# Value products of eight heads into both halves of one PSUM bank, with twelve probability slots and one transposed output buffer

## The chip, the cores and the metric

The kernel runs on one core of a Trainium2 chip. A core has five engines that each work through their own list of instructions in order: TensorE (PE, matmuls and transposes), VectorE (DVE), ScalarE (ACT), GpSimd (POOL) and SyncE (SP, which here only issues DMAs). They meet through semaphores. Matmul results land in PSUM, eight banks of 128 partitions x 512 float32; everything else is in the on-chip buffer. The metric is the time of one launch on the device in microseconds (us), lower is better.

## The reference

One post-norm decoder layer, 16 sequences of 256 tokens, width 256, 16 heads of 16:

```python
x = layernorm(x + self_attention(x))             # q, k RMS-normalised, rotary, causal softmax
x = layernorm(x + cross_attention(x, ctx))       # causal softmax, key mask
x = layernorm(x + ffn(x))                        # RMS norm, light (128) and heavy (1024) hidden units, gelu
# attention, per head:
attn = softmax(where(causal, -inf, q @ k.T * scale))
out  = attn @ v
```

The router of the feed-forward part selects 256 of 256 tokens, so every token goes through both paths, and the kernel computes them as nine chunks of 128 hidden units.

## The kernel before

All 16 sequences are run as a software pipeline, unrolled, one step per sequence. In step i the self-attention (called 1) of sequence s = i, the cross-attention (called 2) of c = i-1, the tail of the cross-attention of f = i-2 and the feed-forward of l = i-3 are in flight together. PE's list of a step has four phases of 16 heads each, and `phase` (line 590) places other work before head h of a phase ("position h"):

- **S1** and **S2**: `scores(1, s, h)` and `scores(2, c, h)`, scores with queries on the partitions, from which DVE takes the row maxima (L869).
- **T1** and **T2**: `scores_t(1, s, h)` and `scores_t(2, c, h)`, the transposed scores less the maxima. Each head fills a bank of a ring of three. ACT takes the exponential (L728) into `pr`, POOL zeroes the masked triangle there (L1176), and PE multiplies the result by the values.

The product is `values(a, b, gr)` (line 508): four heads at a time, each on its own strip of 32 columns of the array, so that the four output strips fill the 128 partitions of `bank3`. It uses columns 0 to 255 of the bank, first the upper keys (256 columns), then the lower keys (128 columns), and a float32 matmul shows as two records in the trace, so that a group of four heads is 16 records. ACT copies a finished group into `oT` (`copy_group`, 256 columns wide), and the next group waits for that copy. Then `out_tokens` transposes `oT` back, DVE divides by the softmax sums (`normalise_heads`, L906 and L909, into `on`), `out_dims` transposes `on` (L367), ACT copies it into `onT`, and `out_proj` applies the output weights. From there DVE adds the residual (L918), takes statistics (L925 to L931), POOL takes the root (L1166), DVE writes the normalised `x` (L946).

Positions of this kernel: the groups 0, 1 and 2 stand at positions 7, 11 and 15 of T1 and T2; group 3 of the self-attention stands at position 2 of T2, behind `k2` (position 1); group 3 of the cross-attention at position 3 of the next S1, behind `transpose_x1` (position 1) and ahead of `q2` (position 4). `out_tokens` follows at position 4 (self) and 5 (cross), `out_dims` at 8 and 10, `out_proj` at 10 and 12. `pr` has eight slots; ACT's exponential of head h waits until the group that read the slot last is done. ACT's list holds, among the exponentials of T1, a copy of `xnh` after head 13 (L674), and among those of T2 the copy of `nat2k` before head 3, of `onT` before head 9, and the squares of the next q and k (L815) before heads 5 and 10. DVE splits q and k of the cross-attention into three bfloat16 parts (L853, L856, L858, tiles `rest` and `nat2`): k just ahead of `normalise_heads(1)`, q ahead of head 5 of the maxima in S1, with `normalise_heads(2)` ahead of head 7. POOL takes the root for `x1` between the masks of heads 12 and 13 of T2.

Of the kernel before, what the change touches and what calls it, by code (L numbers as in the profile page):

```python
# [56 lines left out]
NG = H // HG  # L57
FCH = 9
# [5 lines left out]
def build(nc, io):  # L64
# [4 lines left out]
    with ctx:  # L69
# [51 lines left out]
        pr = sb("pr", [P, 2 * HG, 3 * P])  # L121
        oT = [None] + [sb(f"oT{a}", [P, NG, T]) for a in (1, 2)]
# [89 lines left out]
        def iterations(step):  # L212
            for i in range(-2, B + 4):
# [3 lines left out]
                 if 0 <= turn[2] < B]  # L217
        RING = (0, 1, 2)
# [121 lines left out]
        def _(pe):  # L340
# [89 lines left out]
            def hidden(b, j):  # L430
# [9 lines left out]
                elif j == 1:  # L440
                    if live(b + 1):
                        pe.wait_ge(s_oT[2], NG * (b + 2))
# [41 lines left out]
            def transpose_max(a, b):  # L484
# [3 lines left out]
                else:  # L488
                    if live(b - 3):
                        pe.wait_ge(s_g, FCH * (b - 3) + LIGHT)  # L490
                    if live(b - 2):
                        pe.wait_ge(s_oT[2], NG * (b - 1))
                    wait(pe, s_oT[1], NG * b)
# [14 lines left out]
            def values(a, b, gr):  # L508

                pe.wait_ge(s_prob[a], H * b + HG * (gr + 1))  # L510
                if gr == 0:
# [3 lines left out]
                    elif live(b + 1):  # L515
                        pe.wait_ge(s_oT[1], NG * (b + 2))
# [5 lines left out]
                for key in range(2):  # L522
                    for j in range(HG):
                        h = HG * gr + j
                        out = bank[OT_BANK][VW * j:VW * (j + 1), :]
                        if key == 0:
                            mm(out[:, 0:T], v[:, 0, h, :], pr[:, h % (2 * HG), 0:T], True, False, True)
                        else:
                            last = mm(out[:, P:T], v[:, 1, h, :], pr[:, h % (2 * HG), T:3 * P], False, True, True)
                last.then_inc(s_pv[a], 1)  # L530

            def out_tokens(a, b):

                pe.wait_ge(s_oT[a], NG * (b + 1))
                for t in range(TT):
# [26 lines left out]
                    for gr in range(NG):  # L562
                        last = nc.tensor.transpose(bank[TOK_BANK[a][t]][:, gr * P:(gr + 1) * P],
                                                   oT[a][:, gr, t * P:(t + 1) * P], idf[:, :])
# [33 lines left out]
            def step(i):  # L598
# [9 lines left out]
                if live(f):  # L608
                    add(OUT2_AT[0], values, 2, f, NG - 1)
# [37 lines left out]
                if live(s):  # L647
                    add(K2_AT, k2, s)
                    add(OUT1_AT[0], values, 1, s, NG - 1)
# [11 lines left out]
                if live(c):  # L661
                    for gr in range(NG - 1):
                        add(HG * gr + VALUES_AFTER, values, 2, c, gr)
# [8 lines left out]
        def _(act):  # L672
# [3 lines left out]
            def copy_v(a, b):  # L676
                act.wait_ge(s_v[a], b + 1)

                wait(act, s_pv[a], NG * (b - 1) if a == 1 else NG * b)
# [12 lines left out]
            def copy_group(a, b, gr):  # L692
                act.wait_ge(s_pv[a], NG * b + gr + 1)

                wait(act, s_ott[a], TT * b)
                copy(oT[a][:, gr, :], bank[OT_BANK][:, 0:T]).then_inc(s_oT[a], 1)
# [19 lines left out]
            def exponential(a, b, h):  # L716
                act.wait_ge(s_st[a], H * b + h + 1)

                if h >= 2 * HG:
                    act.wait_ge(s_pv[a], NG * b + h // HG - 1)  # L720
                elif a == 1:
                    wait(act, s_pv[2], NG * (b - 1) - 2 + h // HG + 1)
                    wait(act, s_pv[1], NG * b)
                elif live(b + 1):
                    act.wait_ge(s_pv[1], NG * (b + 1) + 3 + h // HG)
                else:
                    act.wait_ge(s_pv[2], NG * (b - 1) + 3 + h // HG)
                nc.scalar.activation(pr[:, h % (2 * HG), :], ring_bank("T", a, b, h)[:, 0:3 * P], ACT.Exp, scale=HD ** -0.5)\  # L728
# [24 lines left out]
            def step(i):  # L753
                s, c, f, l = i, i - 1, i - 2, i - 3

                if live(f):
# [555 lines left out]
```

## Time and profile before

| | |
|---|---|
| median of 3 runs | 1029.55 us (1028.53 to 1033.22) |
| profiled execution | 1031.08 us, of which the span of the profile is 1029.3 us |
| PE busy | 921.1 us, 89% |
| DVE busy | 734.1 us, 71% |
| ACT busy | 490.1 us, 48% |
| POOL busy | 466.4 us, 45% |

The span is what the profile covers from its first to its last instruction. Busy is the union of an engine's instructions. The ends of matmuls are modelled, and they overlap in the pipeline of the array; how long a stretch of matmuls holds the engine is read from the start of its first matmul to the start of the matmul behind it. A name like `L342` is the line of a helper through which nearly all matmuls go, so matmuls are told apart by their tiles: `pr,va1a`, `pr,va1b` (self) and `pr,va` (cross) are the value products, `ctxT,wk` is `k2`, `x1T,wq` is `q2`, `idf,x` is `transpose_x1`, `idf,oT` is `out_tokens`, `idf,on` is `out_dims`, `wo,onT` is `out_proj`, `stk1q,stk1k` and `stk2q,stk2k` are `scores_t`, `stk1k,stk1q` and `stk2k,stk2q` with `cmaskb,idb` are `scores`.

### The profile page before, as it was taken

How to read it: one execution, taken by the hardware profiler on the slowest of the kernel's cores; microseconds unless marked ns; L12 is line 12 of the kernel's file. 1: busy time of each engine (PE TensorE's matmuls, PEld its weight loads, DVE VectorE, ACT ScalarE, POOL GpSimd, SP SyncE). 2: the span in 40 equal slices, each digit the busy share in tenths (PEclk: the TensorE clock that was granted, in tenths of full speed). 3: DMA queues.
4: the chain of work that ended last, by engine and by line, in shares of the span. 5: the costliest groups of instructions: out<-in, count | busy, mean ns of one | idle time of the engine just before them, and what ended most of it. 6: DMA issues, size and time to landing. Idle time of an engine off the chain costs nothing.

```text
span 1029.3 us, 21587 instructions
## 1 busy us (share of the span) xinstructions
PE 921.1 (89%) x7776; PEld 711.1 (69%) x7776; DVE 734.1 (71%) x1843; ACT 490.1 (48%) x1047; POOL 466.4 (45%) x883
## 2 busy tenths in 40 slices
PE   2565898899999999999999999999999999998886
PEld 2333565587877778786878777787868786766675
DVE  8645858687787877777878878777777788563612
ACT  1131161645555564636465555546374655445343
POOL 2150454545546363546455564635464554233221
PEclk9666799999999999999999999999999999999989
DMA  3629356554729183554546280937556462804000
GB/s 104 82 70 148 63 63 79 79 74 70 97 48 106 39 107 61 81 87 64 84 75 93 52 116 24 110 57 89 79 64 95 62 85 47 111 13 64 21 1 21
DMA packets 79643, 74.22 MB, mean 72 GB/s; under 512 B 8592, under 2 KB 78896, under 8 KB 79536
## 3 DMA queue, kind: packets, MB, share of 16 engines
q1 hardware_dynamic: 75872, 68.90, 46.6%
q10 hardware_dynamic: 3664, 3.94, 1.7%
q8 instruction: 62, 1.02, 0.5%
q14 instruction: 45, 0.37, 0.2%
HBM read 17.49 MB, written 4.20 MB: 21 GB/s over the span
## 4 chain that ended last, share of the span: by engine, by line
PE 61%; DVE 17%; issue 9%; POOL 4%; ACT 3%; DMA 3%; ACTq 1%; SPq 0%; POOLq 0%; DVEq 0%
PE bank L342 56%; PE bank L367 4%; DVE mx L869 3%; POOL pr L1176 3%; DMA y<-in_b 2%; ACT pr L728 2%; DVE x L946 1%; DVE rest L853 1%; DVE y L918 1%; DVE st L925 1%; DVE ss L971 1%; DVE nat2q L858 1%; DVE on L909 1%; DVE rden L906 1%; ACT sq L815 1%
## 5 line engine op out<-in xcount | busy, mean ns | idle before, releaser
L728 ACT ACTIVATE pr<-bank 128x384 f32<-128x384 f32 x512 | 242.5, 499 | 205.5 <-PE bank L342 205.2
L869 DVE TENSOR_REDUCE mx<-bank 128x3 f32<-128x384 f32 x512 | 268.6, 552 | 92.8 <-PE bank L342 89.2
L1176 POOL TENSOR_SCALAR_AFFINE_SELECT pr<-pr 128x256 f32<-128x256 f32 x512 | 225.3, 448 | 214.6 <-ACT pr L728 210.8
L342 PE MATMUL bank<-w,g 128*128 128x256 f32 x576 | 170.8, 389 | 1.1 <-ACT g L740 1.1
L342 PE MATMUL bank<-cmaskb,idb 128*128 128x256 bf16 x512 | 145.7, 285 | 28.5 <-DMA stk1k<-nat1k 14.6
L740 ACT ACTIVATE g<-bank,b 128x256 f32<-128x256 f32 x144 | 68.3, 475 | 112.3 <-PE bank L342 111.8
L1200 POOL TENSOR_TENSOR xTlow<-xT,xThigh 128x512 fp32r<-128x512 f32 x16 | 21.2, 1327 | 174.7 <-ACT xThigh L674 174.7
L342 PEld LDWEIGHTS bank<-w,g 128*128 128x128 f32 x576 | 89.6, 190 | 5.2 <-ACT g L740 1.5
L342 PE MATMUL bank<-stk1k,stk1q 97*128 97x128 bf16 (+1 forms) x512 | 88.6, 259 | 0.0
L342 PEld LDWEIGHTS bank<-cmaskb,idb 128*128 128x128 bf16 x512 | 50.4, 98 | 52.6 <-DVE mx L869 22.2
L342 PE MATMUL bank<-stk1q,stk1k 100*128 100x256 bf16 (+1 forms) x512 | 79.9, 254 | 4.5 <-DMA stk1q<-mT 3.1
L342 PE MATMUL bank<-stk2k,stk2q 97*128 97x128 bf16 (+1 forms) x512 | 82.3, 246 | 0.0
L342 PE MATMUL bank<-stk2q,stk2k 100*128 100x256 bf16 (+1 forms) x512 | 74.8, 251 | 1.9 <-ACT pr L728 0.9
L246 POOL TENSOR_TENSOR qc<-qn,ropeC 128x256 f32<-128x256 f32 x60 | 49.9, 831 | 50.0 <-DVE qn L998 32.6
L342 PE MATMUL bank<-xnh,w1h 128*128 128x256 f32 x288 | 69.1, 321 | 2.3 <-DVE y L918 2.1
L342 PEld LDWEIGHTS bank<-stk1q,stk1k 100*128 100x128 bf16 x512 | 42.3, 100 | 38.3 <-ACT pr L728 8.6
L342 PE MATMUL bank<-wo,onT 128*128 128x256 f32 x256 | 63.3, 391 | 2.5 <-ACT onT L674 2.5
L342 PEld LDWEIGHTS bank<-stk2k,stk2q 97*128 97x128 bf16 x512 | 50.5, 99 | 20.8
L1166 POOL TENSOR_TENSOR rstd<-ve,minus_half 128x2 f32<-128x2 f32 x48 | 33.4, 695 | 63.1 <-DVE ve L931 63.1
L342 PE MATMUL bank<-pr,va 128*32 128x256 f32 (+1 forms) x1024 | 56.7, 340 | 5.5 <-POOL pr L1176 5.3
L342 PEld LDWEIGHTS bank<-stk1k,stk1q 97*128 97x128 bf16 x512 | 53.5, 104 | 9.9 <-issue 0.3
L674 ACT ACTIVATE oT<-bank 128x256 f32<-128x256 f32 x128 | 49.9, 390 | 20.4 <-PE bank L342 14.6
(143 smaller groups left out, 1792.1 us busy)
## 6 DMA issues: line engine op xcount, KB each, us to landing
stk1q<-nat1q SPq DMA_DIRECT2D x96, 128.0 KB, 4.7
stk1k<-nat1k SPq DMA_DIRECT2D x96, 128.0 KB, 6.7
stk2k<-nat2k SPq DMA_DIRECT2D x96, 128.0 KB, 4.6
stk2q<-nat2q SPq DMA_DIRECT2D x96, 128.0 KB, 6.1
xT<-in_xT SPq DMA_DIRECT2D x16, 256.0 KB, 2.8
x<-in_x SPq DMA_DIRECT2D x16, 256.0 KB, 6.8
ctxT<-in_ctxT SPq DMA_DIRECT2D x16, 256.0 KB, 3.0
out_x<-x SPq DMA_DIRECT2D x16, 256.0 KB, 6.5
```

The lines of the kernel that those rows point to most:

```text
L246: ops.tensor_tensor(qc[:, t, s * D:(s + 1) * D].rearrange("p (h d) -> p h d", d=HD), qn[:, t, s * D:(s + 1) * D].rearrange("p (h d) -> p h ...
L342: return nc.tensor.matmul(out, lhsT, rhs, start=start, stop=stop, skip_group_check=check)
L367: last = nc.tensor.transpose(bank[k][:, c * T + t * P:c * T + (t + 1) * P], src[:, t, c * P:(c + 1) * P], idf[:, :])
L674: return nc.scalar.activation(out, in_, ACT.Copy)
L728: nc.scalar.activation(pr[:, h % (2 * HG), :], ring_bank("T", a, b, h)[:, 0:3 * P], ACT.Exp, scale=HD ** -0.5)\
L740: nc.scalar.activation(g[:, j, :], bank[HIDDEN_BANK[j % 2]][:, 0:T], ACT.Gelu, bias=b1[:, j:j + 1])\
L815: nc.scalar.activation(sq[:, t, :], bank[QK1_BANK[t]][:, :], ACT.Square).then_inc(s_sq, 1)
L853: V.tensor_tensor(rest[:, :], bank[SPLIT_BANK[a][s]][:, :], n[:, 0, :], ALU.subtract)\
L869: V.tensor_reduce(mx3[:, h, :], scored[:, 0:3 * P].rearrange("p (k t) -> p k t", k=3), AX.X, ALU.max, negate=True).then_inc(s_mx[a], 1)
L1166: G.tensor_tensor(out, base, minus_half[:, 0:w], ALU.pow)\
L1176: G.affine_select(out=slot, in_=slot, compare_op=ALU.is_ge, fill=0.0, base=0, pattern=[[0, 2], [1, P]], channel_multiplier=-1).then_inc(s_ ...
L1200: G.tensor_tensor(xTp[1][:, :, :], xT[:, :, :], xTp[0][:, :, :].bitcast(f32), ALU.subtract)\
```

## The change

`values` now takes eight heads ("a part"): two groups of four, the second into columns 256 to 511 of the same bank, with one wait ahead of both and one semaphore step behind both. `copy_part` copies a part in one instruction of 512 columns. Part 0 stands at position 11 of T1 and T2, part 1 where group 3 stood. `pr` has twelve slots that are handed out round robin over all T phases, and `oT` is one buffer for both attentions. ACT copies part 0 ahead of head 14 of T1 and of head 13 of T2, and part 1 where it copied group 3. No matmul is added or left out.

```diff
+GH = 2
+SLOTS = 12
-        pr = sb("pr", [P, 2 * HG, 3 * P])
-        oT = [None] + [sb(f"oT{a}", [P, NG, T]) for a in (1, 2)]
+        pr = sb("pr", [P, SLOTS, 3 * P])
+        oT = sb("oT", [P, NG, T])
+        turns_t = [turn[1:] for turn in turns if turn[0] == "T"]
+        def slot(a, b, h):
+            return pr[:, (H * turns_t.index((a, b)) + h) % SLOTS, :]
+        def wait_slot(eng, a, b, h):
+            tile = H * turns_t.index((a, b)) + h - SLOTS
+            if tile >= 0:
+                a0, b0 = turns_t[tile // H]
+                eng.wait_ge(s_pv[a0], GH * b0 + tile % H // (H // GH) + 1)
...
-            def values(a, b, gr):
-                pe.wait_ge(s_prob[a], H * b + HG * (gr + 1))
-                if gr == 0:
+            def values(a, b, part):
+                pe.wait_ge(s_prob[a], H * b + H // GH * (part + 1))
+                if part == 0:
...
-                    pe.wait_ge(s_oT[a], NG * b + gr)
+                    pe.wait_ge(s_oT[a], GH * b + part)
...
+                for gr in range(NG // GH):
+                    for key in range(2):
+                        for j in range(HG):
+                            h = H // GH * part + HG * gr + j
+                            out = bank[OT_BANK][VW * j:VW * (j + 1), gr * T:(gr + 1) * T]
...
-                    add(OUT2_AT[0], values, 2, f, NG - 1)
+                    add(OUT2_AT[0], values, 2, f, 1)
...
-                    for gr in range(NG - 1):
-                        add(HG * gr + VALUES_AFTER, values, 1, s, gr)
+                    add(VALUES_AFTER[0], values, 1, s, 0)
...
+            def copy_part(a, b, part):
+                act.wait_ge(s_pv[a], GH * b + part + 1)
+                if a == 1:
+                    wait(act, s_ott[2], TT * (b - 1))
+                    wait(act, s_ott[1], TT * b)
+                else:
+                    wait(act, s_ott[2], TT * b)
+                    wait(act, s_ott[1], TT * (b + 2) if live(b + 1) else TT * B)
+                groups = slice(part * (NG // GH), (part + 1) * (NG // GH))
+                copy(oT[:, groups, :], bank[OT_BANK][:, :].rearrange("p (g t) -> p g t", g=NG // GH)).then_inc(s_oT[a], 1)
...
-                        if h % HG == 0 and h >= 2 * HG:
-                            copy_group(1, s, h // HG - 2)
+                        if h == COPY_HALF_AT[0]:
+                            copy_part(1, s, 0)
...
-VALUES_AFTER = 7
+VALUES_AFTER, COPY_HALF_AT = (11, 11), (14, 13)
```

The change moves PE's instructions in three kinds of place. The first is S1, on PE, between the transposes of `x1` and `q2` (tiles `x1T`, `wq2`). Before:

```order
L342 MATMUL bank3<-pr,va2 32x256 [waits outT_copied2,probs_ready2]
L342 MATMUL bank3<-pr,va2 32x256 x3
L342 MATMUL bank3<-pr,va2 32x128 x4
L342 MATMUL bank0<-cmaskb,idb 128x2x128 [waits max_ready1]
L342 MATMUL bank0<-stk1k,stk1q 128x128
L342 MATMUL bank0<-stk1k,stk1q 128x256
L342 MATMUL bank6<-x1T,wq2 128x256 [waits x1T_copied]
L342 MATMUL bank6<-x1T,wq2 128x256 x3
```

The same place on PE now, with part 1 of the cross-attention:

```order
L356 MATMUL bank3<-pr,va2 32x256 [waits outT_copied2,probs_ready2]
L356 MATMUL bank3<-pr,va2 32x256 x3
L356 MATMUL bank3<-pr,va2 32x128 x4
L356 MATMUL bank3<-pr,va2 32x256 x4
L356 MATMUL bank3<-pr,va2 32x128 x4
L356 MATMUL bank0<-cmaskb,idb 128x2x128 [waits max_ready1]
L356 MATMUL bank0<-stk1k,stk1q 128x128
L356 MATMUL bank0<-stk1k,stk1q 128x256
L356 MATMUL bank6<-x1T,wq2 128x256 [waits x1T_copied]
L356 MATMUL bank6<-x1T,wq2 128x256 x3
```

Eight more value matmuls, of heads 8 to 11, stand ahead of `q2`.

The second place is the end of T1 on PE, from head 14 to `k2` (tiles `ctxT`, `wk2`). Before:

```order
L342 MATMUL bank0<-stk1q,stk1k 128x256 [waits exp_ready1]
L342 MATMUL bank0<-stk1q,stk1k 128x128
L342 MATMUL bank3<-pr,va1b 32x256 [waits outT_copied1,probs_ready1]
L342 MATMUL bank3<-pr,va1b 32x256 x3
L342 MATMUL bank3<-pr,va1b 32x128 x4
L342 MATMUL bank1<-stk1q,stk1k 128x256 [waits exp_ready1]
L342 MATMUL bank1<-stk1q,stk1k 128x128
L342 MATMUL bank2<-stk2q,stk2k 128x256 [waits exp_ready1,max_loaded2]
L342 MATMUL bank2<-stk2q,stk2k 128x128
L342 MATMUL bank5<-ctxT,wk2 128x256 [waits dve_rest1,ctxT_loaded]
```

The same place on PE now:

```order
L356 MATMUL bank0<-stk1q,stk1k 128x256 [waits exp_ready1]
L356 MATMUL bank0<-stk1q,stk1k 128x128
L356 MATMUL bank1<-stk1q,stk1k 128x256 [waits exp_ready1]
L356 MATMUL bank1<-stk1q,stk1k 128x128
L356 MATMUL bank2<-stk2q,stk2k 128x256 [waits exp_ready1,max_loaded2]
L356 MATMUL bank2<-stk2q,stk2k 128x128
L356 MATMUL bank5<-ctxT,wk2 128x256 [waits dve_rest1,ctxT_loaded]
```

Group 2 is gone from between heads 14 and 15; its heads are now in part 1, behind `k2`.

The third place is T2 on PE, from head 6 to `out_dims` (tiles `idf`, `on1`). Before:

```order
L342 MATMUL bank2<-stk2q,stk2k 128x256 [waits exp_ready2]
L342 MATMUL bank2<-stk2q,stk2k 128x128
L342 MATMUL bank3<-pr,va2 32x256 [waits outT_copied1,va_ready2,probs_ready2]
L342 MATMUL bank3<-pr,va2 32x256 x3
L342 MATMUL bank3<-pr,va2 32x128 x4
L342 MATMUL bank0<-stk2q,stk2k 128x256 [waits exp_ready2]
L342 MATMUL bank0<-stk2q,stk2k 128x128
L367 MATMUL bank5<-idf,on1 128x128 [waits dve_rest2,on_ready1]
```

The same place on PE now:

```order
L356 MATMUL bank2<-stk2q,stk2k 128x256 [waits exp_ready2]
L356 MATMUL bank2<-stk2q,stk2k 128x128
L356 MATMUL bank0<-stk2q,stk2k 128x256 [waits exp_ready2]
L356 MATMUL bank0<-stk2q,stk2k 128x128
L381 MATMUL bank5<-idf,on1 128x128 [waits dve_rest2,on_ready1]
```

Group 0 is gone from ahead of `out_dims`; its heads are in part 0, at position 11, behind `out_proj`.

## Rows read from the trace of the kernel before

**Rows 1.** The page: the span.

```profile
span 1029.3 us, 21587 instructions
```

**Rows 2.** Windows: stretch, its length, busy us and counts by engine, PE clock, DMA.

```profile
489.24:498.66 9.42, 8.82 (x82) 7.48 (x82) 8.53 (x20) 4.90 (x9) 7.86 (x14) 1.00 0.80 117
498.66:518.70 20.04, 20.04 (x153) 17.08 (x154) 15.03 (x37) 6.91 (x13) 5.85 (x8) 1.00 0.45 80
```

**Rows 3.** Waits of PE in one step, 489 to 545.4: us, times, longest.

```profile
PE bank L367 <- DVE on L909: 0.6, 1, 0.6
PE bank L367 <- DVE x L946: 0.4, 1, 0.4
```

**Rows 4.** The chain that ended last, from 480 to 560: start, us, what.

```profile
482.92 0.60 ACT sq L815
...
489.24 0.66 PE bank L367 x4
489.90 3.74 PE bank L342 x36
...
494.14 0.69 DVE rest L853
...
498.66 0.66 PE bank L367 x4
```

**Rows 5.** Timeline of PE around one group of four heads.

```profile
466.03 0.33 PE L342 MATMUL bank<-stk1q,stk1k 100*128 100x256 bf16 x2
466.29 0.86 PE L342 MATMUL bank<-pr,va1b 128*32 128x256 f32 x16
466.53 0.62 PE L342 MATMUL bank<-pr,va1b 128*32 128x256 f32 x12
467.08 0.34 PE L342 MATMUL bank<-stk1q,stk1k 100*128 100x256 bf16 x2
467.25 0.65 PE L342 MATMUL bank<-w,g 128*128 128x256 f32 x2
```

**Rows 6.** Timeline from head 11 of T1 to head 2 of T2.

```profile
470.10 0.34 PE L342 MATMUL bank<-stk1q,stk1k 100*128 100x256 bf16 x2
471.87 0.63 ACT L674 ACTIVATE xnh<-bank 128x512 fp32r<-128x512 f32 x1
472.35 0.92 ACT L728 ACTIVATE pr<-bank 128x384 f32<-128x384 f32 x2
472.95 0.79 POOL L1176 TENSOR_SCALAR_AFFINE_SELECT pr<-pr 128x256 f32<-128x256 f32 x2 [0.47 <-ACT pr L728]
474.67 0.86 PE L342 MATMUL bank<-pr,va1b 128*32 128x256 f32 x16
475.46 0.34 PE L342 MATMUL bank<-stk2q,stk2k 100*128 100x256 bf16 x2
```

**Rows 7.** Timeline of T2, and of S1 from group 3 to `q2`.

```profile
475.83 0.49 ACT L728 ACTIVATE pr<-bank 128x384 f32<-128x384 f32 x1 [0.57 <-PE bank L342]
476.22 0.59 ACT L674 ACTIVATE nat2k<-bank 128x512 bf16<-128x512 f32 x1
480.03 0.66 PE L367 MATMUL bank<-idf,on 128*128 128x128 f32 x4
487.13 0.69 POOL L1166 TENSOR_TENSOR rstd<-ve,minus_half 128x2 f32<-128x2 f32 x1
488.35 0.84 DVE L946 TENSOR_SCALAR x<-y,mv,rstd 128x256 f32<-128x256 f32 x2
490.38 0.86 PE L342 MATMUL bank<-pr,va 128*32 128x256 f32 x16
491.46 1.89 PE L342 MATMUL bank<-x1T,wq 128*128 128x256 f32 x8
```

**Rows 8.** Groups of ACT's instructions: busy us, mean ns, idle before.

```profile
L674 ACT ACTIVATE oT<-bank 128x256 f32<-128x256 f32 x128 | 49.9, 390 | 20.4 <-PE bank L342 14.6 <-issue 5.7
L674 ACT ACTIVATE onT<-bank 128x512 f32<-128x512 f32 x32 | 18.9, 592 | 7.3 <-PE bank L367 7.3
```

More of the change, by code:

```diff
@@ L441, in hidden @@
                     if live(b + 1):
-                        pe.wait_ge(s_oT[2], NG * (b + 2))
+                        pe.wait_ge(s_oT[2], GH * (b + 2))
                     else:
@@ L491, in transpose_max @@
                     if live(b - 2):
-                        pe.wait_ge(s_oT[2], NG * (b - 1))
-                    wait(pe, s_oT[1], NG * b)
+                        pe.wait_ge(s_oT[2], GH * (b - 1))
+                    wait(pe, s_oT[1], GH * b)
                 for t in range(TT):
@@ L515, in values @@
                     elif live(b + 1):
-                        pe.wait_ge(s_oT[1], NG * (b + 2))
+                        pe.wait_ge(s_oT[1], GH * (b + 2))
                     elif live(b - 2):
@@ L519, in values @@
                 else:
-                    pe.wait_ge(s_oT[a], NG * b + gr)
+                    pe.wait_ge(s_oT[a], GH * b + part)
                 v = values_of(a, b)
[L522 to L529, printed above, removed]
+                for gr in range(NG // GH):
[3 more added lines that the diff above has]
+                            out = bank[OT_BANK][VW * j:VW * (j + 1), gr * T:(gr + 1) * T]
+                            if key == 0:
+                                mm(out, v[:, 0, h, :], slot(a, b, h)[:, 0:T], True, False, True)
+                            else:
+                                last = mm(out[:, P:T], v[:, 1, h, :], slot(a, b, h)[:, T:3 * P], False, True, True)
                 last.then_inc(s_pv[a], 1)
             def out_tokens(a, b):
-                pe.wait_ge(s_oT[a], NG * (b + 1))
+                pe.wait_ge(s_oT[a], GH * (b + 1))
                 for t in range(TT):
@@ L648, in step @@
                     add(K2_AT, k2, s)
-                    add(OUT1_AT[0], values, 1, s, NG - 1)
+                    add(OUT1_AT[0], values, 1, s, 1)
                 if live(i + 2):
@@ L661, in step @@
                 if live(c):
-                    for gr in range(NG - 1):
-                        add(HG * gr + VALUES_AFTER, values, 2, c, gr)
+                    add(VALUES_AFTER[1], values, 2, c, 0)
                 phase((lambda h: scores_t(2, c, h)) if live(c) else None, others)
@@ L677, in copy_v @@
                 act.wait_ge(s_v[a], b + 1)
-                wait(act, s_pv[a], NG * (b - 1) if a == 1 else NG * b)
+                wait(act, s_pv[a], GH * (b - 1) if a == 1 else GH * b)
                 copy(values_of(a, b)[:, :, :, 0:HD], bank[V_BANK[a]][:, :].rearrange("p (t h d) -> p t h d", t=TT, h=H))\
@@ L690, in copy_out @@
                 copy_dims(onT[a], DIM_BANK[a]).then_inc(s_onT[a], 1)
[L692 to L696, printed above, removed]
+            def copy_part(a, b, part):
[3 more added lines that the diff above has]
+                    wait(act, s_ott[1], TT * b)
+                else:
+                    wait(act, s_ott[2], TT * b)
+                    wait(act, s_ott[1], TT * (b + 2) if live(b + 1) else TT * B)
+                groups = slice(part * (NG // GH), (part + 1) * (NG // GH))
+                copy(oT[:, groups, :], bank[OT_BANK][:, :].rearrange("p (g t) -> p g t", g=NG // GH)).then_inc(s_oT[a], 1)
             def copy_x1(b):
@@ L717, in exponential @@
                 act.wait_ge(s_st[a], H * b + h + 1)
[L719 to L728, printed above, removed]
+                wait_slot(act, a, b, h)
+                nc.scalar.activation(slot(a, b, h), ring_bank("T", a, b, h)[:, 0:3 * P], ACT.Exp, scale=HD ** -0.5)\
                     .then_inc(s_exp[a], 1)
@@ L754, in step @@
                 s, c, f, l = i, i - 1, i - 2, i - 3
-                if live(f):
-                    copy_group(2, f, NG - 2)
                 if live(c):
@@ L760, in step @@
                 if live(f):
-                    copy_group(2, f, NG - 1)
+                    copy_part(2, f, 1)
                 if live(c):
@@ L796, in step @@
                         if h == COPY1_AT[2]:
-                            copy_group(1, s, NG - 1)
+                            copy_part(1, s, 1)
                         if h == COPY1_AT[3]:
@@ L803, in step @@
                     if live(c):
-                        if h % HG == 0 and h >= 2 * HG:
-                            copy_group(2, c, h // HG - 2)
+                        if h == COPY_HALF_AT[1]:
+                            copy_part(2, c, 0)
                         exponential(2, c, h)
```

8 lines of the change are left out of this document (3 added, 5 removed).

## The prediction

> **What bounds the kernel now.** I read the chain of waits first. In the steady part it alternates between PE and short passages through the other engines [rows 4]. The windows then show how unevenly PE is loaded: from `out_dims` of the cross-attention in S1 to the start of T1 it is busy for 20.04 of 20.04 us, while from `transpose_x1` (489.24) to that `out_dims` (498.66) it is busy for 8.82 of 9.42 us [rows 2]. The list of waits names where it stands still: once per step for `on` (0.6 us) and once for `x` (0.4 us) [rows 3]. So the step consists of stretches that PE sets, and of stretches that a chain through ACT, DVE and POOL sets, in which PE has as much work as the chain lasts and no more. The change moves PE work between these stretches. What it is worth has to be read stretch by stretch, and the reader is to look for which of them lose work and which gain it. The clock is at its upper level, 2.4 GHz (granted 1.00), in both stretches [rows 2].
>
> **What one merge is worth on PE.** A group of four heads starts 0.26 us after the score tile ahead of it (466.03 to 466.29), where such a tile otherwise holds PE for 0.17 (467.08 to 467.25), so entering costs 0.09. The next tile starts 0.79 after the group's first matmul [rows 5]. Inside, the first pass over 256 columns takes 0.24 (466.29 to 466.53). I take 0.22 for the second and half of that for each of the two passes over 128 columns: 0.24 + 0.22 + 0.11 + 0.11 = 0.68, and the remaining 0.11 are the exit. Four heads more, put behind without entry and exit, need 2 x 0.22 + 2 x 0.11 = 0.65. A part therefore holds PE for 0.79 + 0.65 = 1.44 us behind its entry, or 1.53 with it; two groups take 2 x 0.88 = 1.76. A merge gives 0.23 us, and there are 4 per step and 64 in all. Bounds: below, that the second four heads take a full 0.88; above, 0.65. I take 0.65, since all its passes stand in the group already.
>
> The Trainium skill (TensorEngine Tiling (Array Packing), Key Properties) says that changing the tiling mode drains the array. The gaps of 0.09 and 0.11 at a group's edges agree with that [rows 5]. By that rule alone half of the mode changes would go, and the kernel would get faster; this is the first rival below.
>
> **X1 to `out_dims` in S1: one group becomes one part.** The chain runs from `transpose_x1` over PE's list (36 records of L342, among them group 3 at 490.38 and `q2` at 491.46) to the split of q on DVE at 494.14 and over `normalise_heads` to `out_dims` at 498.66 [rows 4, 7]. PE takes its list in order: everything in part 1 stands ahead of `q2`. Behind `q2`, ACT's `nat2q`, DVE's split, two maxima, two reciprocals and two multiplications follow as a chain, and `out_dims` waits for its end (0.6 us [rows 3]), as it did. So `q2` moves back by 0.65 us, and `out_dims` with it: the wait for `on` stays, since its two sides move together. Behind it comes the stretch in which PE is full [rows 2]; nothing there takes the delay back. Cost: +0.65 per step. ACT's copy of the part (0.59 instead of 0.39 by [rows 8]) lies beside `q2` (1.89 us [rows 7]) and costs nothing.
>
> **T1 and the head of T2: two merges and group 2 moved, gain about zero.** PE reaches head 11 of T1 at 470.10 behind two groups [rows 6]; behind one part it does so 0.23 earlier, 469.87. Then comes `transpose_xn`, and heads 12 to 15 without the group that filled PE between 14 and 15. These tiles go through a ring of three banks, so PE is now tied to ACT. An exponential starts 0.37 behind its tile (475.46 to 475.83 [rows 6, 7]), ends 0.49 later, and ACT starts one about every 0.37 to 0.39 when it is full (475.83 to 476.22). Counting on from 469.87: exponential 11 at 470.25, 12 at 470.88 (its tile stands behind a tile of 0.17 and `transpose_xn`, four transposes that I put at 0.45 after the 0.66 of such four with their modelled end [rows 4]), 13 at 471.25, `xnh` at 471.62, the copy of part 0 at 472.10 (a 512-wide copy holds ACT for 0.48, 471.87 to 472.35 [rows 6]), exponentials 14 and 15 at 472.58 and 472.95. The mask of 15 ended 0.47 behind its exponential (472.35 + 0.92 = 473.27 against 472.95 + 0.79 = 473.74 [rows 6]); now it ends at about 473.95. PE's last tile of T1 waits for exponential 12, the first of T2 for 13, until 471.80; `k2`, as long as `q2` without its modelled end, holds it for about 1.8, to 473.75, and part 1 can start at 474.0. Group 3 stood at 474.67 [rows 6]. The part ends 1.44 later, and head 2 of T2 starts at 475.45 to 475.48 where it started at 475.46 [rows 6]. The merges (0.46) and the earlier start are used up by waits of PE for the ring (about 0.6). Bounds from both sides: PE without any such wait would be there 0.46 earlier; with the mask of head 15 late by one more mask it would be there 0.4 later. I take 0.
>
> **T2 to `out_dims`: group 0 goes, nothing is gained.** Head 2 of T2 at 475.46 releases exponential 2, that is followed in ACT's list by `nat2k` at 476.22, and this by the split of k on DVE, then `normalise_heads`, and `out_dims` starts at 480.03 [rows 6, 7]: 4.57 us of chain. PE reached `out_dims` just then because group 0 (0.88) filled the time. Without it PE stands there for about 0.9 us. The transposes of `oT` at position 4 now wait for a copy of 0.59 behind `nat2k`, 0.08 more than PE has time for; the chain over DVE covers that, and I take 0.02.
>
> **T2 to X1: 0.** From `out_dims`, `qk1` for the next sequence but one goes to the squares on ACT at 482.92, and from there over DVE (the sums, the residual, statistics, Newton steps) to `x` at 488.35 and the transposes at 489.24 [rows 4, 7]. PE had groups 1 and 2 in that time (1.76) and waited 0.4; it has part 0 (1.53), waits about 0.6, and the chain is as long. One step of it moves: head 12 comes 0.65 later behind the larger part, ACT has no copy between exponentials 11 and 12 any more (0.26), and POOL's root, behind the mask of head 12, would end at about 488.2 instead of 487.82 [rows 7]. DVE is ready for `x` at 488.35. That cover is 0.1 us thick; if it is gone each step pays up to 0.3.
>
> **Sum.** 0.65 + 0 + 0.02 + 0 = 0.67 us per step. Steps 2 to 16 have the S1 stretch, 15 times: 10.0 us. At both ends of the program the phases stand alone; a part more on the last chain costs 0.65, a copy less ahead of the loads of the feed-forward weights gives about that back. I take 0.4 together. The profiled execution was 1031.08 us for a span of 1029.3 [rows 1], so the changed one would be 1041.5. That execution lies 1.5 above the median of the three runs; against the median the forecast is 1040.0.
>
> **Rivals.**
> First, the merges show in full: PE is the busiest engine and 64 x 0.23 = 14.7 us go, 1014.8 us. For it speaks that PE is full over 20 us of each step; against it, that no group stands in those 20 us, and that every group that goes stands ahead of a chain that PE waits for anyway. Chance 0.07.
> Second, the ends of T1 and T2 give back what S1 pays: if the chain at the end of T1 is looser than I counted, so that PE is 0.46 ahead at head 2 of T2, that goes through the chain behind it whole. Then 0.67 - 0.46 = 0.2 per step, or 3 us; with a shortened split of q (it runs beside POOL's rotation and is stretched by it) also nothing. 1027 to 1034, centre 1031. Chance 0.12.
> Third, one more wait takes hold: POOL's root for `x1` comes late by the full 0.3, and the mask of head 15 by 0.4, so that `x` and part 1 move. It decides as soon as exponential 12 of T2 starts later than about 486.7. Then 1.3 to 1.4 per step, 1051. Chance 0.09.
> Within my own case lies that the merge gives nothing inside the array: 0.88 instead of 0.65 in S1, 1043.5.
>
> **Chances and range.** My case has 0.72, its own range 1036 to 1045. The range that is to hold the time 8 times in 10 is 1033 to 1047: it takes in a small part of the second and of the third rival. A measurement of this kernel tells from no change what is more than about 0.5%, 5.1 us, so 1024.4 to 1034.7 is the same. Slower by more: 0.72 + 0.09 = 0.81, less a little for the low end of my case, 0.80. Same: 0.13. Faster: 0.07.
>
> **What would show it.** In the changed profile: from `transpose_x1` to `out_dims` 10.07 instead of 9.42 us; a step of 57.1 instead of 56.4 us; a part with 1.44 us from its first matmul to the next tile; PE's wait for `on` at two places per step, the new one in T2 near 0.9; its wait for `x` near 0.6 instead of 0.4 or a like time for exponential 13 just ahead; new waits for `pr` of ACT at the end of T1, 0.4 to 0.6 in sum; PE busy for less and ACT for about 64 x 0.19 = 12 us less, without a gain. I am wrong if the stretch from the first tile of T1 to head 2 of T2 is shorter than now by more than 0.2 us, if PE waits less for `on` in S1 than now, or if a stretch in which it is full gets shorter.

## The result and the profile after

The changed kernel takes 1053.26 us (median of 3 runs, 1052.33 to 1053.41) against 1029.55 us before (1028.53 to 1033.22). The ratio is 1.0219, with a 95% interval of 1.0179 to 1.0259. It is slower, as forecast, but by 23.7 us and not by 10.4, and outside the range. Whether it is slower by 2% or more the interval leaves open. Both profiled executions, 1053.26 and 1031.08 us, differ by 22.2 us, and so do their spans; the working below goes by these.

The page's span, which answers to [rows 1]:

```profile
span 1051.5 us, 21397 instructions
```

A steady step, from the transposes of `x1` to the next, takes 57.62 us instead of 56.41. The windows of the changed kernel cut one such step at `transpose_x1`, `out_dims` in S1, the first tile of T1, `k2`, head 2 of T2, `out_dims` in T2 and the next `transpose_x1`. The columns are those of [rows 2], and the first two lines answer to them:

```profile
496.80:507.06 10.26, 9.47 (x97) 7.92 (x97) 8.93 (x20) 5.09 (x9) 8.70 (x16) 1.00 0.96 122
507.06:527.09 20.03, 20.03 (x152) 17.08 (x153) 15.02 (x37) 6.93 (x13) 5.16 (x7) 1.00 0.37 72
527.09:537.21 10.12, 9.44 (x89) 6.64 (x88) 8.43 (x22) 6.92 (x15) 6.72 (x15) 1.00 0.02 4
537.21:540.69 3.48, 3.48 (x44) 2.48 (x42) 2.42 (x7) 2.32 (x6) 1.75 (x5) 1.00 0.66 121
540.69:545.26 4.57, 3.83 (x30) 2.73 (x26) 3.04 (x8) 3.34 (x8) 2.42 (x4) 1.00 1.15 124
545.26:554.42 9.16, 8.72 (x81) 6.70 (x82) 6.57 (x22) 5.75 (x14) 4.50 (x11) 1.00 0.61 66
```

The same cuts of the kernel before, behind those of [rows 2]:

```profile
518.70:529.05 10.35, 10.23 (x105) 6.97 (x104) 8.60 (x23) 7.72 (x18) 7.11 (x15) 1.00 0.02 4
529.05:531.87 2.82, 2.82 (x29) 2.00 (x26) 2.33 (x7) 1.79 (x5) 1.31 (x4) 1.00 0.43 104
531.87:536.45 4.58, 4.35 (x46) 3.15 (x42) 3.04 (x8) 3.25 (x8) 2.80 (x6) 1.00 1.16 125
536.45:545.65 9.20, 8.80 (x83) 6.62 (x81) 6.83 (x22) 5.98 (x15) 4.71 (x12) 1.00 0.72 80
```

| stretch | forecast | measured |
|---|---|---|
| `transpose_x1` to `out_dims` in S1 | +0.65 | +0.84 |
| `out_dims` to T1 | 0 | -0.01 |
| T1 to `k2` | about -0.65 | -0.23 |
| `k2` to head 2 of T2 | about +0.65 | +0.66 |
| head 2 to `out_dims` in T2 | +0.02 | -0.01 |
| `out_dims` to the next `transpose_x1` | 0 | -0.04 |
| step | +0.67 | +1.21 |

Two terms are off: S1 by 0.2 us, and T1 by 0.4. The reader is to see in the third line that PE's busy time in T1 fell by 0.79 us while the stretch fell by 0.23: the rest became waiting. The waits of PE in that step (496.8 to 554.4), which answer to [rows 3], name it:

```profile
PE bank L381 <- DVE on L916: 1.3, 2, 0.8
PE bank L356 <- ACT pr L739: 0.8, 3, 0.3
PE bank L356 <- POOL pr L1183: 0.3, 1, 0.3
```

The chain of waits over S1, which answers to [rows 4], shows the first term as one number. PE's piece behind `transpose_x1` was 3.74 us with 36 records and is 4.39 with 52, that is 0.65 longer:

```profile
496.80 0.66 PE bank L381 x4
497.46 4.39 PE bank L356 x52
...
502.35 0.69 DVE rest L860
503.06 0.64 DVE nat2q L863
...
507.06 0.66 PE bank L381 x4
```

The wait for `on` now stands at two places, 0.79 us in S1 (ahead of 507.06) and 0.48 in T2 (ahead of 545.26), and the one for `x` is gone. The wait of 0.3 for POOL's mask is new in T1. The timeline of the changed kernel at the end of T1, which answers to [rows 5, 6]; its three masks are those of heads 5, 6 and 7, behind POOL's root:

```profile
531.14 0.69 POOL L1173 TENSOR_TENSOR rr<-ssm,minus_half 128x2 f32<-128x2 f32 x1
531.79 1.75 POOL L1183 TENSOR_SCALAR_AFFINE_SELECT pr<-pr 128x256 f32<-128x256 f32 x3
533.60 1.51 PE L356 MATMUL bank<-pr,va1a 128*32 128x256 f32 x32 [0.29 <-POOL pr L1183]
535.04 0.34 PE L356 MATMUL bank<-stk1q,stk1k 100*128 100x256 bf16 x2
536.58 0.34 PE L356 MATMUL bank<-stk1q,stk1k 100*128 100x256 bf16 x2 [0.25 <-ACT pr L739]
537.21 1.94 PE L356 MATMUL bank<-ctxT,wk 128*128 128x256 f32 x8
539.25 1.51 PE L356 MATMUL bank<-pr,va1a 128*32 128x256 f32 x32
540.69 0.34 PE L356 MATMUL bank<-stk2q,stk2k 100*128 100x256 bf16 x2
```

And the kernel before at that place, with groups 0 and 1 and the same three masks:

```profile
522.72 0.86 PE L342 MATMUL bank<-pr,va1a 128*32 128x256 f32 x16
522.75 0.70 POOL L1166 TENSOR_TENSOR rr<-ssm,minus_half 128x2 f32<-128x2 f32 x1
523.40 1.76 POOL L1176 TENSOR_SCALAR_AFFINE_SELECT pr<-pr 128x256 f32<-128x256 f32 x3
525.74 0.86 PE L342 MATMUL bank<-pr,va1a 128*32 128x256 f32 x16
```

A part holds PE for 1.44 us, as worked out (533.60 to 535.04). Part 0 has to wait for the mask of head 7, as group 1 had. Before, that mask ended at 525.16, which is 6.47 us behind the first tile of T1 (518.69), and group 1 began 0.58 later. In the changed kernel it ends at 533.54, 6.45 behind the first tile of T1 (527.09): it did not move. But with group 0 gone from ahead, PE is there 0.83 us earlier, counted in the same way (its wait left out). The cover is used up, and 0.29 are waited. Part 1 starts 0.25 us nearer to `out_dims` of S1 than group 3 did, where 0.67 was forecast.

### The profile page after: what moved, and what is told of

Read it like the earlier page. It is cut to its first block, busy times and chain, and to the rows that moved or that the text cites. A ratio compares the mean times of both kernels' runs of the same rounds, so it can differ in the third digit from the quotient of the medians.

```text
span 1051.5 us, 21397 instructions
## 1 busy us (share of the span) xinstructions
PE 927.4 (88%) x7776; PEld 718.8 (68%) x7776; DVE 735.1 (70%) x1843; ACT 485.4 (46%) x983; POOL 460.4 (44%) x883
## 4 chain that ended last, share of the span: by engine, by line
PE 50%; DVE 24%; issue 11%; POOL 5%; ACT 3%; DMA 2%; ACTq 1%; SPq 0%; POOLq 0%; DVEq 0%
PE bank L356 45%; DVE mx L876 5%; PE bank L381 5%; POOL pr L1183 3%; DVE x L953 2%; DVE rest L860 2%; DMA y<-in_b 2%; DVE on L916 1%; DVE rden L913 1%; DVE y L925 1%; DVE st L932 1%; ACT pr L739 1%; POOL rr L1173 1%; DVE nat2q L863 1%; DVE ss L978 1%
## 5 line engine op out<-in xcount | busy, mean ns | idle before, releaser
L739 ACT ACTIVATE pr<-bank 128x384 f32<-128x384 f32 x512 | 232.7, 501 | 224.4 <-PE bank L356 221.5
L1183 POOL TENSOR_SCALAR_AFFINE_SELECT pr<-pr 128x256 f32<-128x256 f32 x512 | 220.7, 446 | 234.2 <-ACT pr L739 232.7
L356 PE MATMUL bank<-wo,onT 128*128 128x256 f32 x256 | 66.6, 406 | 2.5 <-ACT onT L687 2.5
L260 POOL TENSOR_TENSOR qc<-qn,ropeC 128x256 f32<-128x256 f32 x60 | 46.5, 775 | 48.7 <-DVE qn L1005 30.9
L356 PEld LDWEIGHTS bank<-stk2q,stk2k 100*128 100x128 bf16 x512 | 38.1, 99 | 38.0 <-issue 19.1
L356 PE MATMUL bank<-xnl,w1h 128*128 128x256 f32 x288 | 57.9, 283 | 0.0
```

Source lines behind the costliest of these rows:

```text
L260: ops.tensor_tensor(qc[:, t, s * D:(s + 1) * D].rearrange("p (h d) -> p h d", d=HD), qn[:, t, s * D:(s + 1) * D].rearrange("p (h d) -> p h ...
L356: return nc.tensor.matmul(out, lhsT, rhs, start=start, stop=stop, skip_group_check=check)
L739: nc.scalar.activation(slot(a, b, h), ring_bank("T", a, b, h)[:, 0:3 * P], ACT.Exp, scale=HD ** -0.5)\
L1183: G.affine_select(out=diagonal, in_=diagonal, compare_op=ALU.is_ge, fill=0.0, base=0, pattern=[[0, 2], [1, P]], channel_multiplier=-1).the ...
```

## The experiments

Steps are from one `transpose_x1` to the next in the steady part. Times are medians with their range, ratios are to the kernel before.

**Slots and buffer without a merge.** The changed kernel with four groups:

```diff
-GH = 2
+GH = 4     # positions 7, 11, 15 and copies as before; 12 slots, one oT
```

> Twelve slots and the one transposed output buffer alone: the products stay in groups of four at positions 7, 11, 15 and behind, with copies of 256 columns. Theory 1 (the loss comes from where the eight-head parts stand in PE's list): time of before, 1029 to 1031 us, a step of 56.4 us. Rival (the shared buffer or the slots bring a wait of their own): 1040 to 1053 us, with new waits of ACT for the oT or pr tiles.

Measured: 1029.74 us (1027.6 to 1034.09), ratio 1.0004 (0.9988 to 1.002), step 56.41. Slots and buffer cost nothing that these runs can tell; the loss belongs to the parts.

**Parts in the self-attention alone.**

```diff
-GH = 2
+GH = (None, 2, 4)     # parts for the self-attention, groups for the other
```

> Parts of eight heads for the self-attention alone, the cross-attention in groups of four. Theory 1: only the end of T1 and the head of T2 change, where the changed kernel loses 0.40 us per step (wait for the mask of head 7, waits for the ring of three banks at heads 15 and 0), so 0.4 x 14 = 5.6, 1035 us, and a stretch from the transposes of x1 to out_dims in S1 of 9.42 as before. Rival (losses of the two attentions are one loss, for instance of the wide copies on ACT): about half of 23.7, 1041 us.

Measured: 1040.39 us (1035.73 to 1041.45), ratio 1.0093 (1.0063 to 1.0122); the profiled execution has 1035.73. The step is 56.83, +0.42, and S1 is 9.41, unchanged: step and stretch are as theory 1 has them, while the median lies 5 us above its 1035, at the 1041 of the rival. The execution of 1035.73 had a mean granted clock of 0.956, the three of 1040 to 1041 had 0.946 to 0.952, so the time as a whole can't decide between the two expectations, and the step does.

**Parts in the cross-attention alone.**

```diff
-GH = 2
+GH = (None, 4, 2)
```

> Parts of eight heads for the cross-attention alone. Theory 1: the stretch from the transposes of x1 to out_dims in S1 grows from 9.42 to 10.26 (0.65 for four heads more ahead of q2, 0.19 because DVE's split of q then meets POOL's rotation), T2 stays within 0.1, and the last two steps, which have no qk1 and v1 to fill PE, lose 1 to 2 us each: 0.8 x 13 + 4 = 14 to 18, 1043 to 1048 us. Rival (half of the total each): 1041 us.

Measured: 1049.22 us (1043.61 to 1049.98), ratio 1.0175 (1.0143 to 1.0208), step 57.24, +0.83, with 10.29 from `transpose_x1` to `out_dims`; the time is 1 us above the forecast 1043 to 1048. The two halves add up to 1.25 per step, the whole change has 1.21. So there are two separate costs: T1 with the head of T2, and S1.

**`q2` ahead of the part in S1.**

```diff
-X1T_AT, OUT2_AT, Q2_AT = 1, (3, 5, 10, 12), 4
+X1T_AT, OUT2_AT, Q2_AT = 1, (4, 5, 10, 12), 3
     # ACT copies nat2q ahead of the part
```

> The changed kernel with q2 at position 3 of S1 and part 1 behind it at position 4, and on ACT the first bfloat16 part of q copied ahead of the part's copy. Theory 1 (the split of q is a chain that starts at q2, and part 1 ahead of it delays it): the stretch to out_dims falls from 10.26 to about 9.5, where PE's own work fills it, the wait for on at that place goes from 0.8 to under 0.2, and the time falls by 0.7 x 15 = 10, to 1042 us. Rival (that stretch is long because PE has more work in it): no change, 1053 us, and the stretch stays at 10.2.

Measured: 1058.5 us (1053.87 to 1059.53), ratio 1.0269 (1.0239 to 1.0298), step 58.05: a miss, the wrong way. `q2` did start 1.35 us behind `transpose_x1` instead of 2.87, but DVE's list holds the split of q behind the maximum of head 4, whose score tile now stands behind the part. The split's first step came 5.95 us behind `transpose_x1`, where it was 5.55.

**The same with the split one maximum earlier, and the same two edits in the kernel before.**

```diff
-QN_AT, NORM2_AT, SPLITQ_AT, ... = (1, 2), 7, 5, ...
+QN_AT, NORM2_AT, SPLITQ_AT, ... = (1, 2), 7, 4, ...
```

> As the run before (q2 at position 3 of S1, part 1 at 4), and DVE's split of q one head earlier, ahead of the maximum of head 4, whose score tile stands behind part 1 in PE's list. Theory 1 (the delay of out_dims in S1 comes from everything that stands ahead of the split of q in the lists of PE and DVE): now neither the part nor a score tile behind it is ahead of the split; the stretch from the transposes of x1 to out_dims falls from 10.68 in the run before, and from 10.29 in the changed kernel, to 9.5 to 9.7, and the time to about 1053 - 0.7 x 13 = 1044 us. Rival (DVE and POOL set that stretch by their own work, not by order): it stays at 10.2 to 10.7 and the time at 1053 to 1058.

> The same three edits in the kernel before: q2 ahead of group 3 of the cross-attention, its first part copied ahead of the group, the split of q ahead of the maximum of head 4. Theory 1: the wait of 0.6 for on goes in each step, the stretch falls from 9.42 to 8.8 to 9.0, the step from 56.41 to 55.9, the time to 1022 to 1024 us. Rival (the split, meeting POOL's rotation earlier, is stretched by as much): 1028 to 1031 us.

Measured in the changed kernel: 1051.91 us (1046.27 to 1053.76), ratio 1.0216 (1.0186 to 1.0246), step 57.56, S1 10.25. In the kernel before: 1026.03 us (1022.97 to 1027.79), ratio 0.9958 (0.9939 to 0.9976), step 56.33, S1 9.40. PE's waits in one step, first of the changed kernel so edited, then of the kernel before so edited:

```profile
PE bank L356 <- ACT pr L739: 0.8, 3, 0.3
PE bank L381 <- DVE on L916: 0.5, 1, 0.5
PE bank L578 <- ACT oT L687: 0.3, 1, 0.3
PE bank L356 <- POOL pr L1183: 0.3, 1, 0.3
```

```profile
PE bank L367 <- DVE x L946: 0.4, 1, 0.4
PE bank L342 <- POOL pr L1176: 0.2, 1, 0.2
```

In both the wait for `on` in S1 is gone, and in both the stretch is as long as it was (10.25 against 10.26, 9.40 against 9.42). So S1 has a second bound that lies just under the first: PE's own list, with a wait for the copy of `x1T` ahead of the weights of the earlier `q2` (0.36), and in the changed kernel one for the copy of the part (0.34). The part lengthens both. The reordering did not give the expected time back in either kernel: the changed one keeps its stretch, as the rival of its expectation has it, and the other gets 0.08 us per step where 0.5 was expected. The kernel before with it is the fastest of all that ran.

**POOL's rotation cut to 2 of 16 heads, in both kernels.** Part of the computation is left out in both: the rotary products of 14 heads.

```diff
-    ops.tensor_tensor(qc[:, t, s * D:(s + 1) * D] ..., ropeC ... [P, H, HD], ALU.mult)
+    ops.tensor_tensor(qc[:, t, s * D:s * D + 2 * HD] ..., ropeC ... [P, 2, HD], ALU.mult)
     # and the other products and the sum likewise
```

> The changed kernel with POOL's rotation of the next q and k cut to 2 of 16 heads (the rest of qc, of the rotated halves and of qr is left out, in all but the first sequence). If DVE's split of q is stretched because POOL's rotation runs beside it, the cast of nat2q falls from 640 ns to 430 and the subtraction from 1100 to 690, and the stretch to out_dims from 10.29 to about 9.7, so a step of 57.0 instead of 57.6. Rival (the 0.2 beyond the four heads come from PE or ACT): both keep their length, and the stretch stays at 10.3.

> The kernel before with POOL's rotation cut to 2 of 16 heads (part of the computation is left out), as the baseline for the same cut in the changed kernel, where the step lost 0.31 us and the split of q fell from 1100 to 693 ns. Theory 1 (in the changed kernel the split of q runs beside the rotation in a stretch in which it did not before): here the second half of the split falls too, since it met the rotation before, by 0.4, but the cast of nat2q is at 0.43 already and stays; x to out_dims is 0.4 shorter at most, that is the changed kernel lost nothing in this stretch that the cut gives back to it alone except the 0.2 of the cast. Rival (the rotation costs both kernels alike): step lower by 0.3, the same as in the changed kernel, and the difference of the two steps stays at 1.2 us.

Measured, one execution each: in the changed kernel 1049.78 us, step 57.31 (-0.31), S1 9.94; in the kernel before 1032.36 us, step 56.72 (+0.31), S1 9.72. Less work on POOL makes the kernel before slower, which neither theory of the second run expected. The durations of DVE's two steps of the split say why. Each line gives minimum, median and maximum in ns; first the kernel before, whole and with the light rotation, then the changed kernel, whole and with it:

```profile
L856 DVE CAST nat2q<-rest x16: 427/428/651, 109.6 to 945.3; 128x512 bf16<-128x512 f32 x16
L858 DVE TENSOR_TENSOR nat2q<-rest,nat2q x16: 693/1101/1103, 110.3 to 945.8; 128x512 bf16<-128x512 f32 x16
```

```profile
L858 DVE CAST nat2q<-rest x16: 426/1147/1149, 107.2 to 946.1; 128x512 bf16<-128x512 f32 x16
L860 DVE TENSOR_TENSOR nat2q<-rest,nat2q x16: 691/693/694, 107.6 to 946.5; 128x512 bf16<-128x512 f32 x16
```

```profile
L863 DVE CAST nat2q<-rest x16: 426/640/658, 108.5 to 965.0; 128x512 bf16<-128x512 f32 x16
L865 DVE TENSOR_TENSOR nat2q<-rest,nat2q x16: 693/1100/1104, 109.2 to 965.5; 128x512 bf16<-128x512 f32 x16
```

```profile
L865 DVE CAST nat2q<-rest x16: 426/716/726, 106.3 to 960.2; 128x512 bf16<-128x512 f32 x16
L867 DVE TENSOR_TENSOR nat2q<-rest,nat2q x16: 691/693/693, 106.7 to 960.6; 128x512 bf16<-128x512 f32 x16
```

With the light rotation both subtractions fall to 693 ns, but the casts grow, since another instruction of POOL now stands beside them. In the kernel before the cast grows by 0.72 us and the subtraction falls by 0.41, which is the 0.31 that the step lost; in the changed kernel they are +0.08 and -0.41, and the step fell by 0.31. Now S1 can be worked out for both pairs. The cast differs by 640 - 428 = 0.21 us between the whole kernels, and 0.65 for the four heads ahead of `q2` plus 0.21 makes 0.86; measured 0.84. It differs by 716 - 1147 = -0.43 between the light ones: 0.65 - 0.43 = 0.22; measured 9.94 - 9.72 = 0.22. So the 0.65 of the prediction fits both pairs, and the term that was missing is the length of DVE's cast, which depends on what POOL runs beside it. The first expectation had the subtraction right and the cast wrong.

**Part 0 of T1 one head later.**

```diff
-VALUES_AFTER, COPY_HALF_AT = (11, 11), (14, 13)
-MAX2_AT, XNT_AT = 5, 12
+VALUES_AFTER, COPY_HALF_AT = (12, 11), (14, 13)
+MAX2_AT, XNT_AT = 5, 13
```

> The changed kernel with part 0 of the self-attention one head later, at position 12 of T1, and the transposes of xn at 13. Theory 1 (T1 loses 0.29 by the wait for the mask of head 7, and more by the ring at heads 15 and 0): the mask is done by then, the wait of 0.29 goes, part 1 starts 0.3 earlier, the step is 57.3, and the time 1053 - 0.3 x 13 = 1049 us. Rival (the end of T1 is set by ACT's exponentials alone): the wait goes but comes back in the ring waits, 1053 us.

Measured: 1048.86 us (1044.64 to 1050.6), ratio 1.0174 (1.0142 to 1.0206), step 57.28, -0.34; PE's wait for the mask is gone, as theory 1 has it.

**POOL's root out of the way of that mask.**

```diff
-RR2_AT, RSTD3_AT, RSTD1_AT = 5, 3, 13
+RR2_AT, RSTD3_AT, RSTD1_AT = 8, 3, 13
```

> The changed kernel with POOL's root for k of the cross-attention (RR2_AT) between the masks of heads 7 and 8 of T1 instead of 4 and 5, so that the mask of head 7 is not behind it. Theory 1 (the covers at the end of T1): part 0 of T1 loses its wait of 0.3 us for the mask of head 7, and with it the stretch from x to x loses 0.3: step 57.3 instead of 57.63, and steps 14 and 15, where the same kind of wait stands ahead of part 0, lose at most as much; time lower by 3.5 to 5, 1048.5 to 1050. Rival (PE is tied to the ring of three tiles in any case, so that the wait is only the first of several in a row): the wait for the mask goes and those for ACT's exponentials grow by the same 0.3; step 57.55 to 57.65, time within 1 us of the changed kernel.

Measured: 1050.49 us (1046.18 to 1053.69), ratio 1.0208 (1.0183 to 1.0234), step 57.29. The time as a whole moved by less than its own spread, and its median is 0.5 us above what theory 1 had; the step, which repeats to 0.04 in each trace, decides. PE's waits in it:

```profile
PE bank L381 <- DVE on L916: 1.3, 2, 0.8
PE bank L356 <- ACT pr L739: 0.8, 3, 0.3
```

The wait of 0.3 went and no other one grew, so it was on the path in full, and theory 1 holds for the step. Here the mask of head 7 ends 5.64 us behind the first tile of T1, not 6.47: the root was what had held it. About the same 0.33 to 0.34 comes back by moving the part behind the mask or the root behind the mask.

**One merge in T1 only.** The stretches in which the cross-attention's parts cost are left as before, and the one merge stands in T1, where PE was busy for 10.23 of 10.35 us:

```diff
+PARTS = (None, ((0, 4), (4, 12), (12, 16)), ((0, 4), (4, 8), (8, 12), (12, 16)))
+VALUES_AT = (None, (7, 15), (7, 11, 15))
```

> Twelve slots and one oT, but only one merge: of the self-attention, heads 0 to 3 at position 7 of T1, heads 4 to 11 as one part at position 15, heads 12 to 15 at position 2 of T2; the cross-attention has four groups of four at their places in the kernel before. So the only stretch that gets another amount of PE work is T1, in which PE is full, and no part stands ahead of q2, out_dims or x. Theory 1 (a merge is worth its 0.23 us where PE is full and what stands behind it is not on a chain): T1 to k2 0.23 us shorter, step 56.2 instead of 56.41, time 1026 to 1027. Rival (the exponentials of the ring starve behind a part of 1.53 us and the time comes back as waits of PE for pr in the head of T2): step 56.4 or more, time 1029 to 1032.

> The same single merge in T1, and in S1 q2 ahead of group 3 with the split of q one maximum earlier (the two edits that gave the kernel before 0.08 us per step and 1026.0). Theory 1: the two gains stand in different stretches and add up, step 56.1, time 1022 to 1023.5, faster than both kernels. Rival (both are gains in slack that one chain through T2 and S1 takes back): no better than the better of the two alone, step 56.3, 1026.

Measured: 1040.1 us (1036.7 to 1044.53), ratio 1.0108 (1.0085 to 1.0132), step 57.05, +0.64. With the edits of S1: 1035.52 us (1035.05 to 1037.6), ratio 1.007 (1.0056 to 1.0085), step 56.96. Theory 1 is wrong: a merge in T1 doesn't pay but costs, and all 0.64 lie between T1's start and `k2` (10.35 to 10.99). The rival had the side, but neither the size nor the engine: it is POOL's mask and not an exponential that is late. The edits of S1 give 0.09 here and gave 0.08 in the kernel before, so that part of the second expectation holds. The first kernel's timeline there:

```profile
531.78 2.52 POOL L1193 TENSOR_SCALAR_AFFINE_SELECT pr<-pr 128x256 f32<-128x256 f32 x5 [0.25 <-ACT pr L745]
...
533.28 1.51 PE L358 MATMUL bank<-pr,va1a 128*32 128x256 f32 x32 [0.79 <-POOL pr L1193]
```

Without group 1 ahead of them, heads 11 to 14 and `transpose_xn` pass PE sooner, and it waits for the mask of head 11. That mask ends 9.16 us behind the first tile of T1, where it ended 9.18 behind it before. So the part starts when group 2 did, 9.21 against 9.23, and holds PE for the 0.65 of four heads longer: that is the 0.64. In the last heads of T1 the pace is set by ACT and POOL, at 0.4 to 0.5 us for a head (2.52 for 5 masks). The groups between them did not slow T1: they were what PE did while it would have waited. That PE was busy for 99% of the stretch did not show that less work would shorten it.

## Why the prediction was right on the side and wrong on the size

**What one merge is worth on PE.** Right: 1.44 us from a part's first matmul to the next tile. ACT's copies, which answer to [rows 8], fell from 49.9 to 38.9 us in sum, where 12 less was forecast; ACT's busy time as a union fell by 4.7 alone (490.1 to 485.4), and nothing hung on it. PE's busy time was to fall too; it rose from 921.1 to 927.4 us over the program and fell by 0.08 in the steady step (55.05 to 54.97). The modelled ends of tiles run into the waits behind them, so it doesn't show what four merges take out. ACT's copies now:

```profile
L687 ACT ACTIVATE oT<-bank 128x512 f32<-128x512 f32 x64 | 38.9, 608 | 24.2 <-PE bank L356 24.2
```

**S1.** The mechanism was right, the term was too small: 0.65 forecast, 0.84 measured, and the wait for `on` did not stay at 0.60 but grew to 0.79. The working took all behind `q2` as a chain of fixed durations. DVE's cast of q was 428 ns only because it was issued ahead of POOL's instruction: it starts at 494.85, and POOL's second `qr` at 494.90. The changed kernel's timeline:

```profile
501.98 1.43 POOL L272 TENSOR_TENSOR qr<-qc,sq 128x256 f32<-128x256 f32 x2
503.06 0.63 DVE L863 CAST nat2q<-rest 128x512 bf16<-128x512 f32 x1
503.36 0.92 POOL L260 TENSOR_TENSOR qc<-qn,ropeC 128x256 f32<-128x256 f32 x1
```

The cast ends 0.28 us behind the end of POOL's `qr` (503.69 against 503.41). In the kernel before with the light rotation it ends 0.28 us behind the end of an addition of 1.28 us that runs from 493.04 (494.60 against 494.32). The Trainium skill (SBUF — State Buffer, Who interferes with whom) states that a DVE cast in a two-port mode and a GpSimd instruction exclude each other, and that whichever is issued first keeps the other out until it is done. That the cast comes to its end only when POOL is done agrees with both traces; taken in full the rule would have it end its own 0.43 behind POOL's end, and it ends 0.28 behind it. In the runs with the earlier `q2` of the changed kernel the cast also ends 0.28 behind POOL's instruction, at lengths of 0.93 and 0.58 us. The prediction had read this stretching of the split and used it in its second rival alone, with the opposite sign.

**T1 and the head of T2.** This is the step that failed: "PE reaches head 11 of T1 at 470.10 behind two groups [rows 6]; behind one part it does so 0.23 earlier". PE reaches it 0.11 later (7.95 us behind the first tile of T1, before 7.84). The working held only if part 0 could start as soon as PE came to it. Part 0 reads the mask of head 7, which had a cover of 0.58 us and stays where it was, and the merge takes PE there 0.83 earlier. I counted the exponentials and masks from head 11 on, but not those ahead of the part. The step gains 0.34 where that wait is taken away in either of two ways, and 56.41 + 0.65 + 0.21 = 57.27 is then the forecast with the corrected cast; measured 57.28 and 57.29.

**T2.** Both stretches behind head 2 were right to 0.04. The new wait for `on` there has 0.48, forecast 0.9; 0.25 more stand ahead of it as a wait for an exponential. The wait for `x` was forecast near 0.6 and is gone: another one, for an exponential just ahead, has taken its place, which the text had left open.

**The ends.** This is the other half of the miss. Forecast +0.4, and 0.67 for each of four irregular steps, 3.1 in all. Of the 22.2 us, 11 steady steps have 11 x 1.21 = 13.3 (forecast 7.4), and 8.9 are left for the ends. The last two steps ahead of the last `transpose_x1` have 5.7 instead of 2.4, the stretch from the second to the third `transpose_x1` has 2.8 (PE busy there for 2.1 more, at a mean granted clock of 0.91 instead of 0.97), the start -1.3 and the tail 1.6. Of the 3.3 too many in the last two steps nearly all stands in `out_proj`, 1.6 in each, at a lower clock. One of the two steps as windows, with a stretch of two us inside it, of the changed kernel:

```profile
842.59:901.61 59.02, 52.86 (x463) 41.02 (x463) 41.53 (x102) 28.60 (x59) 27.95 (x56) 0.97 0.49 69
...
892.00:894.00 2.00, 1.09 (x5) 0.79 (x4) 0.00 (x0) 1.36 (x3) 0.81 (x2) 0.81 1.14 120
894.00:896.00 2.00, 2.00 (x6) 1.60 (x5) 0.00 (x0) 0.00 (x0) 0.00 (x0) 0.50 1.12 114
```

The same step before, whole and where `out_proj` begins:

```profile
827.74:883.59 55.85, 51.53 (x462) 39.73 (x463) 41.22 (x102) 28.99 (x63) 27.99 (x55) 1.00 0.54 73
...
877.64:879.64 2.00, 2.00 (x20) 1.42 (x21) 0.47 (x1) 0.36 (x1) 0.25 (x1) 1.00 1.18 123
```

In these steps PE has no `qk1` left and waits for `oT`, `on` and `onT` in turn. Before, group 0 stood among these waits, and the clock stayed at 1.00; without it the granted clock falls here from 1.00 to 0.50, that is from 2.4 to 1.2 GHz, and `out_proj` at 893.04 needs 3.4 us to the next tile instead of 1.8. With part 0 of T1 one head later, the first of the two steps keeps 1.00:

```profile
839.72:896.69 56.97, 51.01 (x463) 39.97 (x463) 41.76 (x102) 28.53 (x59) 27.98 (x56) 1.00 0.51 72
```

It is 2.05 us shorter, 0.34 of that by the wait. But it has the same waits of 1.4, 0.25, 0.6 and 0.9 us as the changed kernel, so these alone don't decide whether the clock falls. In all traces of this case: the seven kernels whose cross-attention has groups keep 1.00 in both of these steps; the seven where it has parts lose it somewhere in the second, and two of them, the changed kernel and the one with the late root, in the first as well. That a fall of the clock is what the rest costs is read from `out_proj` in the traces; no run held the clock apart from the waits, and what decides whether it falls stays open. The mean granted clock of the changed kernel's three executions was 0.949 to 0.952, of the kernel before 0.958 in the profiled one.

**The rivals.** The first (merges show in full) fell: T1 to `k2` has 1.11 us less of value products and is 0.23 shorter, and the head of T2 takes 0.66 back. The second fell too, since T1 gave nothing to spare. The third has the nearest time, 1051, but not its mechanism: the mask of head 15 and the root for `x` were in time, and the late mask was one of head 7.

## What to carry to other kernels

Work that stands between the items of a paced chain (exponential, mask) is cover, even where the engine shows 99% busy: before taking it out, compare when each input of what comes next is ready with when the engine would then be there, for the instructions ahead of the merged block as well as behind it. Here the mask had 0.58 us of cover and the engine came 0.83 earlier. A duration that sits on a chain beside another engine's traffic is not a constant; its minimum and maximum over the program show how far it can move. And where work was removed from a place in which the matrix engine already waits several times in a row, the clock fell a level in some of the traces, so the clock of such a place belongs among what is compared.

## What was not expected of the hardware

- Less work on one engine made a kernel slower: with the light rotation the kernel before lost 0.31 us per step, because DVE's cast went from 428 to 1147 ns beside an addition on POOL.
- The granted clock fell to 0.50 behind waits of PE of 1.4, 0.6 and 0.9 us in each of two steps, where it had stayed at 1.00 with one group of 0.86 us among waits of about the same size; `out_proj`, which met the lower level, took 1.6 us longer. With part 0 of T1 one head later the same waits in the first of these steps left it at 1.00.
- Two bounds can lie within 0.02 us of each other: taking away the wait for `on` in S1 (0.6 us) shortened that stretch by 0.02 in the kernel before.
